# Decoder layer: the loop over rows 1 to 3 written out, and the residual added from two PSUM banks

## The reference, cut to what matters

```
x = x + mamba(layernorm(x))            # W_in, causal conv of 4 taps, silu, selective scan with 16 states, gate, W_out
x = x + xattn(layernorm(x), ctx)       # softmax over 154 keys, projections folded into few matrices
x = x + ffn(layernorm(x))              # RMS norm, top-2 of 8 experts, bf16; out = xc16 + combined.astype(bf16)
```

## Time and profile before

| what | value |
|---|---|
| median of 3 runs | 1599.04 us (1598.52 to 1600.43) |
| profiled execution, its own time | 1600.42 us |
| span of the profile, first to last instruction | 1598.6 us |
| mean granted TensorE clock | 0.900 |
| DVE busy | 1374.6 us (86%) |
| PE busy | 1244.0 us (78%) |
| POOL busy | 972.1 us (61%) |
| ACT busy | 931.7 us (58%) |

### The profile page before, as it was taken

How to read it: one execution, slowest core, us unless ns; L and a number is a source line. 1 busy time by engine, 2 the same in 40 slices (tenths; PEclk the granted TensorE clock), 3 DMA queues, 4 the chain that set the end, 5 groups by cost and what they waited for, 6 DMA issues and landing times. The chain is left out here.

```text
span 1598.6 us, 23982 instructions
## 1 busy us (share of the span) xinstructions
PE 1244.0 (78%) x5942; PEld 855.6 (54%) x5942; DVE 1374.6 (86%) x1811; ACT 931.7 (58%) x1388; POOL 972.1 (61%) x529
## 2 busy tenths in 40 slices
PE   4876667779787877898788777798778877886797
PEld 2354445655455545665355545576355545575475
DVE  5599999687899999887799999887799999973697
ACT  3355444244677767625677767814677767722564
POOL 1398888312889879522798978631689879720000
PEclk8879988889799988999899989899889989987799
DMA  6011111401121211311112112221111212220111
GB/s 220 29 47 53 51 50 36 161 3 55 49 80 51 73 60 59 111 46 55 41 57 71 58 54 90 79 78 42 54 47 55 64 47 78 75 95 27 47 59 53
DMA packets 76620, 102.24 MB, mean 64 GB/s; under 512 B 9180, under 2 KB 54117, under 8 KB 76526
## 3 DMA queue, kind: packets, MB, share of 16 engines
q1 hardware_dynamic: 71372, 97.36, 18.8%
q10 hardware_dynamic: 5154, 3.78, 0.7%
HBM read 82.69 MB, written 18.43 MB: 63 GB/s over the span
## 5 line engine op out<-in xcount | busy, mean ns | idle before, releaser
L1773 PE MATMUL ps<-ident,work 128*128 128x128 f32 x1536 | 307.2, 323 | 207.5 <-DVE stage L1386 68.7
L1348 DVE TENSOR_TENSOR_SCAN work<-ps,work 128x1024 f32<-128x1024 f32 x192 | 438.5, 2284 | 24.8 <-ACT ps L960 19.8
L1773 PEld LDWEIGHTS ps<-ident,work 128*128 128x128 f32 x1536 | 193.6, 160 | 342.6 <-DVE stage L1386 119.7
L960 ACT ACTIVATE ps<-dt,a_neg 128x1024 f32<-128x1024 f32 x256 | 285.5, 1117 | 140.7 <-DVE work L1348 84.2
L708 POOL TENSOR_TENSOR work<-dtu,b_bc 128x1024 f32<-128x1024 f32 x128 | 302.0, 2389 | 50.9 <-PE ps L1773 47.0
L1386 DVE SCALAR_TENSOR_TENSOR stage<-ps,c_tok,stage 128x512 f32<-128x512 f32 x384 | 272.1, 734 | 20.7 <-PE ps L1773 18.7
L1795 PE MATMUL ps<-w,work 128*128 (+1 forms) x1024 | 255.0, 395 | 2.5 <-DVE work L1514 2.5
L1795 PEld LDWEIGHTS ps<-w,work 128*128 128x128 f32 x1024 | 198.8, 198 | 41.0 <-issue 3.9
L724 POOL TENSOR_TENSOR stage<-stage,work 128x512 f32<-128x512 f32 x128 | 160.4, 1276 | 56.5 <-ACT work L976 56.5
L1745 PE MATMUL ps<-nfT,w 128*128 128x512 bf16 x512 | 165.0, 421 | 33.8 <-DVE work L1447 19.8
L708 POOL TENSOR_TENSOR work<-dtu,w_out 128x1024 f32<-128x1024 f32 x64 | 149.3, 2355 | 47.8 <-PE ps L1773 47.8
(11 more groups left out here) (169 smaller groups left out, 1957.4 us busy)
## 6 DMA issues: line engine op xcount, KB each, us to landing
b_bc<-b_rows SPq DMA_DIRECT2D x32, 512.0 KB, 3.9
w_out<-b_rows SPq DMA_DIRECT2D x32, 512.0 KB, 4.4
wbc<-combine_rows SPq DMA_DIRECT2D x64, 256.0 KB, 3.6
work<-z_rows SPq DMA_DIRECT2D x8, 1024.0 KB, 6.2
z_rows<-mix SPq DMA_DIRECT2D x24, 256.0 KB, 2.7
stage<-in_x SPq DMA_DIRECT2D x8, 512.0 KB, 4.4
xt<-in_x SPq DMA_DIRECT2D x8, 512.0 KB, 3.9
x_rows<-xt SPq DMA_DIRECT2D x4, 1024.0 KB, 4.3
```

What stands on the lines that cost most here:

```text
L960: act.activation(decay_in(d, alone, opening), dt[:, d, :], ACT.Exp, scale=a_neg[:, bass.ds(it * 2 + (d * N + hf * (N // 2) + par), 1)]).th ...
L1348: dve.tensor_tensor_scan(h, decays, h, 0.0, ALU.mult, ALU.add).then_inc(scan_done, 1)
L1773: mm = pe.transpose(ps[:, a % HT_BANKS, d * P:(d + 1) * P], slot(par, d)[:, a * P:(a + 1) * P], ident[:, :])
```

## The change

1. `over_rows`: the engine loop over rows 1 to 3 becomes a Python loop, so that each engine's program has these rows one after the other, with constants where the row's counter was. The engine loops inside `turns` and in SP's `loads` stay.
2. `finalize`, part 2: `scalar_tensor_tensor` (times 1.0, then add) becomes `tensor_tensor` (add), on the same bf16 data. This holds for both halves of all rows.
3. For the first half, where it lies in the middle of the scan loop (rows 0 to 2's experts, in the written-out state `second`): parts 3 and 4 no longer read `res` from SBUF. ACT copies `res` into PSUM banks 0 and 1 (`bank_res`, 512 columns each), and DVE adds `mix` to it from there (`add_banked`). `bank_res(0)` stands on ACT behind decay 3 and waits for tile 6 of the state before to be taken from bank 0; `bank_res(1)` stands behind the Tanh pair and waits for tile 7. On DVE `add_banked(0)` stands behind the accumulation of tile 7, `add_banked(1)` behind `gate_product(s, 1)`, so both are now behind scan 3.
4. PE, in the first state of the following engine loop's body (hf = 1, par = 0, all three passes of it): before the transposes of tile 0 it waits for `res_summed`, before those of tile 1 for `out_ready`. In the second and third pass both are long set.
5. For the last row's first half (beside no scan) and for all second halves, parts 3 and 4 stay as they were.

```diff
-            with eng.Fori(1, B) as b:
+            for b in range(1, B):
                 phases(phase_between(b))
                 loop(b, b - 1)
...
+                def bank_res(half):
+                    if half == 0:
+                        wait_apart(act, res_loaded, bp * 32 + 16)
+                    wait_apart(act, hT_used, state(b, 1, 0, 1) * SUMMED - 1 + half + HT_CREDIT)
+                    act.activation(ps[:, half, :], res[:, half * 2:half * 2 + 2, :].rearrange("p a d -> p (a d)"), ACT.Copy
+                                   ).then_inc(res_banked, 1)
...
                     decay(b, bp is None, hf, it, par, 3)
...
+                        if second:
+                            bank_res(0)
                         chains[1][1]()
+                        if second:
+                            bank_res(1)
...
-                        dve.scalar_tensor_tensor(mix[:, :], mix[:, :], 1.0, flat16, ALU.mult, ALU.add
-                                                 ).then_inc(mix_added, 1)
+                        dve.tensor_tensor(mix[:, :], mix[:, :], flat16, ALU.add).then_inc(mix_added, 1)
...
+                def add_banked(half):
+                    cols = slice(half * HALF, (half + 1) * HALF)
+                    if half == 0:
+                        dve.wait_ge(mix_added, bp * 2 + 1)
+                    wait_apart(dve, res_banked, bp * 2 + half + 1)
+                    ins = dve.scalar_tensor_tensor(res[:, :, :].rearrange("p a d -> p (a d)")[:, cols], ps[:, half, :], 1.0,
+                                                   mix[:, cols], ALU.mult, ALU.add)
+                    ins.then_inc(out_ready if half else res_summed, 1)
...
                         linear_product(s, par, 0)
                         if second:
-                            for part in range(2, 5):
-                                finalize(0, part)
+                            finalize(0, 2)
                     scan(w, par, 3, decay_in(3, bp is None))
                     accumulate(hf, it, par, 7)
                     if bp is not None:
+                        if second:
+                            add_banked(0)
                         gate_product(s, 1)
+                        if second:
+                            add_banked(1)
...
-                    transposes_of((0, 1))
+                    if bp is not None and hf == 1 and not isinstance(it, int) and par == 0:
+                        pe.wait_ge(res_summed, bp + 1)
+                        transposes_of((0,))
+                        pe.wait_ge(out_ready, bp * 2 + 1)
+                        transposes_of((1,))
+                    else:
+                        transposes_of((0, 1))
```

More of the change, by code:

```diff
@@ L282, in decoder_layer @@
         mix_taken = sem("mix_taken")
+        res_banked = sem("res_banked")
+        res_summed = sem("res_summed")
         out_ready = sem("out_ready")
@@ L396, in phase_between @@
         def phase_between(b):
-            if isinstance(b, int) and b == 0:
+            if b == 0:
                 return Phase(None, 0, False, True, [0, 0, 0])
             before = [n + (b - 1) * m for n, m in zip(total_a, total_both)]
-            if isinstance(b, int):
+            if b == B:
                 return Phase(b - 1, None, True, False, before)
@@ L1073, in body @@
                     decay(b, bp is None, hf, it, par, 3)
+                    second = hf == 1 and isinstance(it, int) and par == 1
                     if bp is None:
@@ L1542, in _ @@
             over_rows(dve, phases, loop)
-            assert links == {"a": LINKS_A * 2, "c": LINKS_C * 2}
+            assert links == {"a": LINKS_A * B, "c": LINKS_C * B}
         @block.tensor
```

## The result

The kernel after takes 1576.3 us, median of 4 runs (1574.5 to 1576.8), against 1598.9 (4 runs) for the kernel before. The ratio is 0.985, with an interval of 0.9835 to 0.9861; applied to the 1599.0 us shown at the start, this is 1574.7, or 24.3 us less (22.2 to 26.4). The forecast was 18.2 less.

What follows compares the result with a forecast made beforehand. DVE was taken to set the pace. Savings of 13.5 + 3.5 + 1.0 + 0.5 - 0.3 = 18.2 us took the profiled 1600.4 to 1582.2; for the runs 1581 was named, range 1575 to 1588.

Steps and rivals of the forecast that it cites:

- What bounds the kernel, and why the additions took 2.7 us: Scan loop: DVE sets the pace; mid-loop, its additions with both inputs in SBUF take turns with POOL's products.
- The mid-loop sums: Middle of the scan loop, three rows: cheaper sums let the next accumulation start 4.5 us earlier; 13.5 us saved (9.9 to 15.6).
- The bf16 addition: Outside the mid-loop: tensor_tensor at 0.69 us instead of 1.21 saves 1.0 at two row ends, 0.5 at the kernel's end.
- rival 1: The bf16 addition keeps its single rate at six places on the path: 3.1 us less gain, 1584; chance 0.12.
- ACT is the new bound, PE's tiles come in time: Behind the mid-loop sums: ACT's queued copies delay the decay, DVE idles 0.7 us; PE's tiles are not last.
- Rival 3: Mid-loop: banks handed over late, DVE also waits for PE's tiles 2 and 3; up to 2 us a row, 1587; chance 0.05.
- The turns, 3.5: Row loop written out: DVE's 1.78 us of idle at each of two turns goes, nothing else last; 3.5 us (0 to 4.0).
- Rival 2: At the turns: writing out rows does nothing, idle moves to x's landing or PE's O; loses 3.5, 1584.5; chance 0.10.
- Rival 4: Scan loop: 12 inner branches back start to miss, 21 us at 1.78 each, 1602, slower than before; chance 0.04.
- Rival 5: More gain, with register operations gone from waits on the path: 1577; chance 0.07.
- register operations: Steady states of the written-out rows: constants replace sums with the row counter; taken as 0, bound 0 to 3 us of gain.

Runs made afterwards that it cites:

- experiment 3: Kernel before with the bf16 addition as tensor_tensor and the two additions to res moved behind scan 3, still from SBUF: 1590.4 us, ratio 0.9948.
- experiment 2: Sum edits apart, each on the kernel before: bf16 addition alone as tensor_tensor, 1597.9 us; only the two additions to res from PSUM, 1587.5 us.
- one_wait: Kernel after, but PE waits for both PSUM additions before tile 0's transposes instead of one before each tile: 1580.4 us, ratio 0.9890 to the kernel before.
- dve_rows: Kernel before with the loop over rows 1 to 3 written out on DVE alone: 1598.8 us, ratio 0.9990.
- one_branch: Kernel after, but rows 1 and 2 in an engine loop and only row 3 written out: 1582.9 us, ratio 0.9901 to the kernel before.
- banks_only: Kernel before with res copied to PSUM and added from there, bf16 addition and row loop kept as they were: 1587.5 us, ratio 0.9922.
- all_written: Kernel after with inner loops over states also written out on PE, DVE, POOL and ACT's scan states: 1564.0 us, ratio 0.9766 to the kernel before.

## Why the prediction was right, and where it was not

- *What bounds the kernel, and why the additions took 2.7 us*: right. Additions with both inputs in SBUF beside POOL's products take 2.71, 2.82 or 2.30; the same additions from PSUM 0.67 (experiment 3).
- *The mid-loop sums, 13.5 (9.9 to 15.6)*: right, 13.4 in the traces. Forecast and measured in the first row: addition 0.87 and 0.86; PSUM additions 0.69 and 0.67; idle for ACT 0.7 and 0.68; 4.5 and 4.46 saved.
- *The bf16 addition, 1.0 at the turns and 0.5 at the end*: right for the size, 0.68 against 1.21 at a row's end, so rival 1 is out, and right for the end (0.54). At the turns it holds only because the rows are written out in the same change: where PE keeps its branch the gain is given back in the phases (experiment 2). The forecast did not see that this term depends on the other. That in the middle of the loop its 0.5 would count by itself was not claimed, and it does not (experiment 2).
- *ACT is the new bound, PE's tiles come in time*: half wrong, without effect on the sum. The tiles come just in time; holding them back by one addition costs 3.8 us in three rows (one_wait against after), and taking ACT's delay away gains nothing measurable. Rival 3 had the right mechanism and a price that did not arise.
- *The turns, 3.5*: the size of DVE's own stall was right, 3.8 in every kernel without it. **The step that failed is the size of the term for writing out the row loop**: I priced it by DVE's idle time alone, said that nothing else was last, took 0 for all the rest, and 3.5 for the whole. Measured are 8.3 to 9.3. Two things were missed. PE's branch at the same place, 4.2 us in work, leaves its projection late and mostly slow, hidden before by DVE's stall; had only DVE's loop been written out, the 3.5 would have been given back (dve_rows). I had seen that its idle would shrink "at the same branch", and did not ask what it did to the length of 15.74. And row ends, the phases behind the turns and the last row together lose 3 us with the loop, which I had put at 0 with up to 3 of gain. The reason that I had given for such a gain, constants in place of the counter, is not what the traces show: the decays that start behind a register operation are 141 before and 139 after. Where these 3 us come from stays open, and so do the 2 us that no stretch behind the opening holds.
- *Rival 2*, that the idle time only moves, is what happens if PE keeps its branch, and is wrong here. *Rival 4* is wrong: no scan shows idle by issue. *Rival 5* (1577) came nearest.
- *The range* was 1575 to 1588, and the measured 1574.7 (with its interval, 1572.6 to 1576.8) lies 0.3 us outside. The low end is 24.0 less than before: the upper bounds of the mid-loop part, the turns and the addition (15.6 + 4.0 + 2.0 = 21.6) and 2.4 of the 3 us for register operations. All upper bounds together (24.6) give 1574.4, which holds the time. That would have been luck: the upper bound of 4.0 for the turns has no room for what PE's branch costs, and the register operations are not where the time went.

## What to carry to other kernels

A stall that several engines share is priced by removing it from all of them: alone on VectorE or on TensorE it was worth nothing that could be told, on both 9 us, more than VectorE's 3.5 us of idle showed. Ask the trace for the loop's own line, since the branch has a record there with its duration on TensorE, though it counts as no work and its idle time was put down to a semaphore. Look for short SBUF additions on VectorE that take as long as a GpSimd product beside them, and give them a PSUM operand or a place where GpSimd is quiet. After a loop is written out for its branch, write out the inner ones as well if the program's size allows it, since here they were worth more than the outer one; what to look for is a register operation between a semaphore and the instruction that waited for it, on an engine that the bounding one waits for.

## What the hardware showed that was not expected

- TensorE's projection of 64 matmuls takes 13.98 us when it follows other matmuls, at a granted clock of 1.00 (full speed, 2.4 GHz); behind 2.49 us of idle 15.74; behind 3.94 us 17.11, with a mean granted clock of 0.61 over its first 8 us. But the length of the idle time does not settle it: behind 3.54 us in one_branch it takes 14.05 at a granted clock of 1.00, behind 4.07 in banks_only 15.44.
- The branch back of the row loop is in work for 4.0 to 5.8 us on TensorE, and for 0.07 where it leaves the loop.
- An engine loop of three passes over two states costs by itself: 12 us went with them, though no branch had left an idle time by issue. A decay on ScalarE starts 0.12 us behind the scan that it waits for, 0.19 to 0.21 with a register operation between the semaphore and the decay.
- The opening of 316 to 320 us, in which only all_written changes anything, differs by up to 4.5 us between executions of kernels that share it, and by 3.3 between two of the same kernel.
